# The gate of a second cross-attention: sigmoid by way of the hyperbolic tangent instead of the exponential and a reciprocal

## What is computed

```python
def _L1_xattn_ref(char_emb, subword_emb, ...):
    ...
    char2sub = jnp.einsum('bqk,bkh->bqh', jax.nn.softmax(scores, axis=-1), V_sub)
    ...
    sub2char = jnp.einsum('bqk,bkh->bqh', jax.nn.softmax(scores2, axis=-1), V_char)
    ...
    gate_in = jnp.concatenate([char2sub, sub2char], axis=-1)
    gate = jax.nn.sigmoid(jnp.einsum('blh,oh->blo', gate_in, Wg) + bg)
    return gate * char2sub + (1 - gate) * sub2char

x = x + _L0_xattn_ref(_layernorm(x, axis=-1), ctx_1024, ctx_1024, ...)
x = x + _L0_ffn_ref(_layernorm(x, axis=-1), ...)      # 6 layers
x = x + _L1_xattn_ref(_layernorm(x, axis=-1), ctx_1024, ...)
x = x + _L1_ffn_ref(_layernorm(x, axis=-1), ...)      # 2 layers
```

## Time and profile before

| what | value |
|---|---|
| time, median of 3 (lowest, highest) | 2159.86 us (2158.65, 2161.14) |
| time of the profiled execution | 2162.79 us |
| its span | 2161.0 us |
| busy: TensorE, VectorE, ScalarE, GpSimd | 96%, 84%, 77%, 64% |
| mean granted TensorE clock | 0.987 |

### The profile page before, as it was taken

The page is one execution under the profiler, slowest core; times in us unless marked ns, Lnnn a source line. Parts: engine busy times, 40 slices in busy tenths (PEclk is TensorE's granted clock), DMA queues, the critical chain, the costliest instruction groups (busy, mean ns, idle before and its releaser), DMA issues. The chain is left out here.

```text
span 2161.0 us, 87976 instructions
## 1 busy us (share of the span) xinstructions
PE 2070.8 (96%) x33646; PEld 1430.2 (66%) x33646; DVE 1825.5 (84%) x4867; ACT 1673.6 (77%) x5828; POOL 1389.0 (64%) x1318
## 2 busy tenths in 40 slices
PE   7989999999999999999999999999999788999998
PEld 4656766667666666666666666666666565666665
DVE  5889988888988889898888889888896587888873
ACT  4767888888888888888888888888887336787784
POOL 1337867777776777777677777767774226666660
PEclk9999999999999999999999999999999988999999
DMA  4001222112211222112221222112221100000000
GB/s 119 5 3 37 76 62 50 46 52 67 61 44 46 72 61 51 43 48 72 63 50 45 53 67 61 44 46 63 50 52 37 31 18 6 14 16 13 15 11 25
DMA packets 144805, 97.03 MB, mean 45 GB/s; under 512 B 61976, under 2 KB 137408, under 8 KB 144384
## 3 DMA queue, kind: packets, MB, share of 16 engines
q1 hardware_dynamic: 143232, 91.02, 16.6%
q10 hardware_dynamic: 1152, 0.26, 0.1%
HBM read 23.11 MB, written 1.05 MB: 11 GB/s over the span
## 5 line engine op out<-in xcount | busy, mean ns | idle before, releaser
L726 PE MATMUL bank<-wqkv,hs 128*128 128x512 f32 x1344 | 658.3, 610 | 5.0 <-ACT arena L1581 2.5
L1972 POOL TENSOR_TENSOR arena<-arena,rnorm 128x512 f32<-128x512 f32 x448 | 455.3, 1045 | 277.7 <-DVE rnorm L259 276.4
L1965 POOL TENSOR_TENSOR arena<-arena 128x512 f32<-128x512 f32 x448 | 565.9, 1273 | 58.0 <-DVE arena L2185 58.0
L1610 ACT ACTIVATE arena<-bank,amx 128x64 f32<-128x64 f32 x1536 | 457.5, 332 | 26.7 <-DVE amx L2242 26.4
L726 PEld LDWEIGHTS bank<-wqkv,hs 128*128 128x128 f32 x1344 | 230.2, 191 | 178.1 <-issue 158.1
L1610 ACT ACTIVATION_READ_ACCUMULATOR arena<-bank,amx 128x1 f32 x1536 | 346.3, 225 | 0.0
L2185 DVE TENSOR_TENSOR arena<-bank,rot 128x256 f32<-128x256 f32 x896 | 334.2, 415 | 0.0
L2180 DVE TENSOR_TENSOR arena<-bank,rot 128x512 f32<-128x512 f32 x448 | 306.7, 685 | 23.6 <-PE bank L726 20.8
L1587 ACT ACTIVATE arena<-bank 128x512 f32<-128x512 f32 x426 | 249.9, 621 | 87.9 <-PE bank L747 87.9
L747 PEld LDWEIGHTS bank<-ident,arena 128*128 128x128 f32 x1792 | 213.3, 142 | 155.4 <-issue 112.4
L1979 POOL TENSOR_TENSOR arena<-arena,ainv 128x512 f32<-128x512 f32 x192 | 200.2, 1043 | 167.7 <-DVE ainv L2250 167.5
(11 more groups left out here) (229 smaller groups left out, 3290.2 us busy)
## 6 DMA issues: line engine op xcount, KB each, us to landing
arena<-arena SPq DMA_DIRECT2D x768, 64.0 KB
wqkv<-in_L_ffn_Wqkv_dram SPq DMA_DIRECT2D x24, 256.0 KB
hs<-z SPq DMA_DIRECT2D x128, 32.0 KB, 2.1
hs<-z SPq DMA_DIRECT2D x128, 31.8 KB, 1.9
fx<-z SPq DMA_DIRECT2D x31, 128.0 KB, 2.2
fx<-z SPq DMA_DIRECT2D x31, 127.0 KB, 2.5
wqkv<-in_L_ffn_Wqkv_dram SPq DMA_DIRECT2D x24, 128.0 KB
w<-in_L_ffn_W_dram SPq DMA_DIRECT2D x6, 341.0 KB
```

The lines of the kernel that those rows point to most:

```text
L726: nc.tensor.matmul(bank[o][:], src[:], wqkv[w][:, off:off + 512], start=True, stop=True).then_inc(AT[name] if part < 2 else AT[name][i], 1)
L1610: ins = nc.scalar.activation(pb[i][0][p % 2][:, h * DH:(h + 1) * DH], bank[3 + g][:, j * DH:(j + 1) * DH], ACT.Exp, bias=amx[p % 2][:, i, ...
L1965: nc.gpsimd.tensor_tensor(t, t, rs[i][c], ALU.add).then_inc(AT["ak" if c else "aq"][i], 1)
L1972: nc.gpsimd.tensor_tensor(t, t, rnorm[p % 2][:, i, HU * c:HU * c + HU].unsqueeze(2).to_broadcast([P, HU, DH]), ALU.mult).then_inc(AT["mk" ...
```

## The change

ScalarE now takes tanh((g + b) / 2), with a bias of b / 2 made once. Since the sigmoid is (1 + tanh(·/2)) / 2, VectorE makes the gate in two operations: `y_m` = (t + 1) · `y_d`, and x = 0.5 · `y_m` + x. The semaphore `gt` counts 2 a pair instead of 4, and all waits on it are rescaled. Parts 0 and 1 are dropped from their places in `y_step`, and the two new ones stand where parts 2 and 3 stood.

```diff
-                nc.scalar.activation(y_nb[:], yb[:, 6:7], ACT.Copy, scale=-1.0).then_inc(YP["we"], 1)
+                nc.scalar.activation(y_hb[:], yb[:, 6:7], ACT.Copy, scale=0.5).then_inc(YP["we"], 1)
...
-                at(act, YP["gt"], 4 * p - 1)
-                nc.scalar.activation(y_e, bank[6][:, 0:256], ACT.Exp, scale=-1.0, bias=y_nb[:, 0:1]).then_inc(YP["ge"], 1)
+                at(act, YP["gt"], 2 * p - 1)
+                nc.scalar.activation(y_e, bank[6][:, 0:256], ACT.Tanh, scale=0.5, bias=y_hb[:, 0:1]).then_inc(YP["ge"], 1)
...
-                at(pool, YP["gt"], 4 * p - 1)
+                at(pool, YP["gt"], 2 * p - 1)
...
-                dve.wait_ge(YP["ge"], p + 1)
-                at(dve, YP["gt"], 4 * p + part)
                 x = base_x[:, 256 * p:256 * p + 256]
                 if part == 0:
-                    ins = nc.vector.tensor_scalar(y_e, y_e, 1e30, 1.0, ALU.min, ALU.add)
-                elif part == 1:
-                    ins = nc.vector.reciprocal(y_e, y_e)
-                elif part == 2:
+                    dve.wait_ge(YP["ge"], p + 1)
                     dve.wait_ge(YP["di"], p + 1)
-                    ins = nc.vector.tensor_tensor(y_m, y_e, y_d, ALU.mult)
+                    at(dve, YP["gt"], 2 * p)
+                    ins = nc.vector.scalar_tensor_tensor(out=y_m, in0=y_e, scalar=1.0, in1=y_d, op0=ALU.add, op1=ALU.mult)
                 else:
+                    dve.wait_ge(YP["gt"], 2 * p + 1)
                     dve.wait_ge(YP["x1"], p + 1)
-                    ins = nc.vector.tensor_tensor(x, x, y_m, ALU.add)
+                    ins = nc.vector.scalar_tensor_tensor(out=x, in0=y_m, scalar=0.5, in1=x, op0=ALU.mult, op1=ALU.add)
                 ins.then_inc(YP["gt"], 1)
...
                 if second >= 0:
                     y_subtract(second)
-                if fourth >= 0:
-                    y_gate(fourth, 0)
                 between(s, 1)
                 if new >= 0:
                     y_project(new, 1)
-                if fourth >= 0:
-                    y_gate(fourth, 1)
                 if second >= 0:
                     y_row_sum(second)
                 if fourth >= 0:
-                    y_gate(fourth, 2)
+                    y_gate(fourth, 0)
                 if second >= 0:
                     y_inverse(second)
                 if fourth >= 0:
-                    y_gate(fourth, 3)
+                    y_gate(fourth, 1)
                 between(s, 2)
```

More of the change, by code:

```diff
@@ L165, in build @@
         y_inv = sb("y_inv", [P, 4])
-        y_nb = sb("y_nb", [P, 1])
+        y_hb = sb("y_hb", [P, 1])
         xbq = sb("xbq", [P, 1])
@@ L944, in group_norm_1 @@
                         pe.wait_ge(LN["xn"], NBLK + n)
-                        pe.wait_ge(YP["gt"], 8 * (n - 7))
+                        pe.wait_ge(YP["gt"], 4 * (n - 7))
                         g_mean(pe, n, n - 8, 2)
```

## The result

The changed kernel takes 2151.1 us in the median of six runs (2148.6 to 2153.3), the kernel before 2160.5 in six beside them; the ratio is 0.9948 with a 95% interval of 0.9937 to 0.9958. That is faster by 9.4 us in the medians, whose quotient is 0.9957, also within the interval; 11.4 was forecast.

A forecast was written before the change was run, and what follows sets the result against it. The gates' stretch was taken as bound by VectorE and round trips through it, TensorE only in between. Terms 1.3 + 0.3 + 1.1 + 2.2 + 3.1 + 3.4 = 11.4 us took the median from 2159.9 to 2148.5 us, range 2143.5 to 2156.

The forecast's parts named there:

- pair 1: Row sum ahead of L902 starts earlier without the reciprocal, less 0.5 for the moved table load; 1.3 us, bounds 0.5 to 1.8.
- pair 2: Row sum can start only 0.3 us earlier, when its exponential ends; 0.3 us, bounds 0 and 1.66.
- pair 3: L338 comes 1.2 us earlier, but TensorE's own queue ahead of L321 is next late; 1.1 us.
- pairs 4 and 5: L338 comes earlier and L321 behind pair 5, which waited 2.35 us, takes it all; 2.2 us, bounds 1.5 to 2.35.
- clock behind pair 5: From L321 to the broadcast's end, clock stays at 2.4 GHz once the idle time shrinks; 3.1 us, bounds 0 and 3.1.
- pairs 6 and 7: Two gates in one chain to L747; gain 3.4 us, between 2.5 at half clock and some 4.2 at full clock.
- Some 1.5 us: VectorE time expected to go at each pair's gate, 12 us for eight pairs, not all of it counting.
- the clock stays: Behind pair 5, with 2.2 of 2.35 us idle gone, the clock was expected to stay at 2.4 GHz; 3.1 us.
- That the clock falls behind pair 5 as before: First rival: the 3.1 us is lost and the last term is 2.5; gain 7.4 us, 2152.5 us; chance 0.23.
- That the waits only change owner: Third rival: exponential, GpSimd and TensorE's queue replace the reciprocal; at most 4 us gained, 2156 to 2160 us; chance 0.12.
- That Tanh is dearer: Fourth rival: Tanh takes longer than the exponential on ScalarE, ahead of the softmax exponential; 2164 us or more; chance 0.03.
- The second, a better clock from L747 on: Second rival: full clock from 1790 to 1801 us too, about 4 us more gain, 2144.5 us; chance 0.12.

The follow-up runs named there:

- e6: The changed kernel run and profiled again, unchanged; median 2149.9 us, ratio 0.9933 to the kernel before.
- e10: The kernel before with the gate's reciprocal cut to 4 of its 256 columns and the TENSOR_SCALAR's limit set to 1.0; ratio 0.9958.
- e8: The kernel before with Tanh in place of the exponential, VectorE's four operations kept, added constant 2.0; ratio 0.9988.
- e4: The changed kernel with the exponential in place of Tanh, VectorE's two operations kept; median 2148.1 us, ratio 0.9928.
- e2: The changed kernel with an extra 128x256 reciprocal put back at its old place for pairs 4 and 5 alone; median 2153.5 us, ratio 0.9953.
- e3: The kernel before with five unused matmuls filling TensorE's wait ahead of L321 behind pair 5; 2160.2 against 2163.1 us, ratio 0.9985.
- e5: The kernel before run and profiled again, unchanged; ratio 1.0000.
- e7: The changed kernel with filling matmuls, four ahead of the L280 before the first gate, five ahead of pair 7's product; median 2150.1 us, ratio 0.9933.
- e1: The changed kernel with an extra 128x256 reciprocal put back at its old place for pairs 6 and 7 alone; median 2151.1 us, ratio 0.9944.

## Why the prediction was right

It named five places, and the clock behind one of them, and the traces have a number for each. The places are differences of the table's columns between before and after, and at pair 2 those of the L280 behind it (30.45 and 28.77).

| term | forecast | measured |
|---|---|---|
| pair 1 | 1.3 | 1.36 |
| pair 2 | 0.3 | 0.32 |
| pair 3 | 1.1 | 1.09 |
| pairs 4 and 5 | 2.2 | 2.39 |
| clock behind pair 5 | 3.1 | 3.12 |
| pairs 6 and 7 | 3.4 | 3.82 (2.83 in e6) |
| sum | 11.4 | 12.10 (11.09 in e6) |

The clock's 3.12 is taken to L1239 of pair 6, which starts at 62.13 and 53.85. The two ratios that were measured, 0.9948 and 0.9933, are 11.2 and 14.5 us of 2160; the forecast is 0.9947. That the first ratio meets it so closely is luck: the medians beside it say 9.4 us, and those of e6 14.7.

One size was low throughout. "Some 1.5 us" a pair is the reciprocal's 1.66 less 0.13 for the fused operations, and leaves out the TENSOR_SCALAR that goes too; VectorE's busy time fell by 14.5 us, 1.8 a pair. It did little harm, since e10 puts the two operations at 0.36 us up to pair 5.

**Pair 1.** The size was right and its working half right. The 1.3 was argued as the reciprocal's time cut down by the moved load. e8 shows that the load's old place had cost VectorE 1.07 us of its own, and that taking it away brings 1.17 us with the reciprocal still there. e10 shows 1.55 us with the reciprocal gone and the load in its old place, e4 1.75 with the two operations. Together, in the change, they bring 1.36: each removes a wait in front of the same row sum, and the load's new place takes 0.39 back, where 0.5 was forecast. The Trainium skill, "ScalarE: Activation LUTs", section "What ACT_TABLE_LOAD costs", adds a drain of 1.38 us to each load. This case doesn't agree: the exponential starts 1.30 us after the start of the load, which takes 1.28.

**Pairs 2 to 5.** What limits each gain was right: the softmax exponential at pair 2, TensorE's own queue at pair 3 (L321 follows L1239 without idle time), and at pairs 4 and 5 TensorE's scores and the exponential in the queue ahead of L338. The gains there don't add up from parts. e2 gives 1.75 us for the reciprocals at pairs 4 and 5 with all else changed, which leaves 0.64 of the 2.39. But e10, which keeps the TENSOR_SCALARs and shortens the reciprocals, gets 2.34 from L321 to L321 (13.08 to 10.74). So the rest of the change counts only as long as the reciprocals fill VectorE's queue.

**The clock.** Shown by e3 and e2 from both sides: filling the idle time without shortening anything kept the clock, and bringing the idle time back lost it. In the four traces with 2.09 us or more idle ahead of L321 it fell, in the eight with 0.55 or less it stayed. What a fall costs isn't fixed, though: after the same wait of 2.35 us the stretch to L280 was 6.02 and 6.03 us in the two traces of the kernel before and 4.80 in e8. So 3.1 us is what this fall costs when it comes at L321 itself, and the kernel before could have had a cheaper one. The step "the clock stays" was the least certain of the forecast, and held.

**Pairs 6 and 7.** The chain was read rightly, and the gain lay between the two bounds, 2.5 and 4.2, but not by the half clock at L1239 of pair 7 that set them. From L1239 of pair 7 to L747, where both gates stand, the kernel before takes 8.57 us (e5: 8.56), the changed one 5.24 and 5.30: 3.3 us less, though L1239 was at or near half clock in all four (1.90 to 2.08 us). That is more than 2.5 because TensorE's own work there ended 0.6 to 0.7 us sooner at the better clock behind it. The rest of the term, from L1239 of pair 6 to that of pair 7, is clock alone: 6.82 us before, 6.33 and 7.26 in the two traces of the changed kernel. The upper bound had a wrong step: it took GpSimd's difference to be hidden, at full clock too. In e7, with L1239 at full rate, the second gate waits for that difference and the term is 3.90. e1 ties 2.17 us of the gain to the reciprocals.

**The rivals.** That the clock falls behind pair 5 as before: no. That the waits only change owner: in part, since the row sum now waits 5.4 us for ScalarE, but this was in the sum. That Tanh is dearer: no, 471 ns. The second, a better clock from L747 on worth some 4 us, is open. From L747 to the end of the span the changed kernel's first profile takes 5.1 us less than before (368.3 against 373.4), as that rival has it, but e6 takes 371.8 and e7 373.7, with the same work. The seven traces with two operations a gate take 368.1 to 373.7 (median 368.6), the five with four operations 369.4 to 373.4 (median 372.0). That leans towards the rival, but the ranges overlap, and so few profiles don't settle it.

## What to carry to other kernels

Price an operation by what waits behind it: the eight reciprocals took 14 us in front of four waits of TensorE, and each place gave back only what the next late input allowed. Look for that input among the buffers too: with one buffer for `y_d`, GpSimd was the next one late at the last gate. Where TensorE is idle for 2 us in otherwise dense work, filling matmuls tell apart what the wait costs and what the clock behind it costs. When an activation function changes, look where its table load moves, since both its old and its new place here held up another engine.

## What the runs showed of the hardware

An idle stretch of 2.67 us ahead of L902 at pair 1 was followed by full clock in every trace of the kernel before (six matmuls in 2.81 or 2.82 us), and one of 2.09 us behind pair 5 by half clock (e2). After one of 2.35 us the half clock began with the first matmul behind it or only some 1 us later (before and e5; e8). The length of the idle stretch alone doesn't tell.

The filling matmuls ahead of the L280 in front of the first gate took away the half clock behind it in both kernels that had them (1.6 us each), though TensorE did nothing useful in the meantime. The same filling 60 us later didn't prevent a fall of some 10 us that came 9 us behind it.

GELU and the hyperbolic tangent followed each other without a table load (L1671 ends at 1722.17, L1805 starts at 1722.55, and the load comes at 1724.07), and the exponential and the hyperbolic tangent too, so the two sets in use both hold the hyperbolic tangent. A function in both sets lets the build put the load at a later activation.
